# Cross attention with scores by head in 64-row halves, two units of scores and maxima by turns, then the value products of two units

## The chip, the cores and the metric

One core of a Trainium2 chip runs the whole program. The metric is the device time of one execution in microseconds (us), less is better.

## The reference

A two-layer Perceiver-like network on 128 query tokens of width 256, with a context of S = 12544 rows of width 256. The part that the change touches is the cross attention of the second layer, 16 heads of 16 columns:

```python
q, k, v = x @ Wq.T + bq, ctx @ Wq.T + bq, ctx @ Wq.T + bq   # projected by a shared weight
scores  = q_h @ k_h.T * 16 ** -0.5        # for each head h: 128 x 12544, fp32 accuracy
p       = softmax(scores, -1)             # over all 12544 keys
x       = x + concat_h(p @ v_h) @ Wo.T + bo
```

Everything before it (a history context, convolutional attention, kernel attention, a mixture of experts) and after it (a retention layer, a low-rank feed-forward) is the same in both kernels.

## The kernel before

Keys and values were projected earlier and lie in device memory (`k_scratch`, a rounded high part and a low part of each key row; `v_scratch`). The 16 heads are worked in NG = 8 pairs. For pair `s` the keys stand in `k_stack[s % 2]`, a tile of 128 partitions by 12544 keys: head 0 of the pair in rows 0 to 48, head 1 in rows 64 to 111. Its rows are three copies of the head's 16 dimensions (high, low, high) and a row of ones (row 32) which carries the negated maximum of each query into the score. `q_max` and `q_stack` hold the queries in the same rows. All these tiles are fp32r, the rounded 32-bit type; `prob` and `vals` are plain fp32, and a product of them is recorded as two matmuls.

TensorE has three kinds of work for a pair:

- **Maxima** (`maximum_group`, L866): queries stationary, keys moving, units of MU = 448 keys. The two heads of a pair are two matmuls in different row halves, into two PSUM banks. VectorE then takes the maxima of both banks in one reduction of 896 columns (`reduce_unit`, L1616). There are 28 units in a pair and 224 in all. `MAX_SLOTS` holds two slots of two banks, and a unit waits until the reduction of the unit two before it is done.
- **Scores** (`scores`, L889): a tile of 128 keys stationary, all 112 rows at once, and 256 moving columns: 128 for each head, with zeros in the rows of the other head. Two tiles fill one bank, and ScalarE turns that bank of 512 columns into `prob` (`exponentials`, L1180). There are 98 tiles and 49 exponentials in a pair, 784 and 392 in all, in three banks.
- **Value products** (`weigh`, L905): 32 columns of `vals` stationary, 128 columns of `prob` moving, into four column groups of 32 partitions in one bank.

When all units of a pair are reduced, VectorE takes the pair's maximum (L1622), TensorE turns it into rows (`turn_maxima`, L876) and ScalarE copies the row into `q_stack` (L1173); then the scores of the pair may start.

The order on TensorE is written out by `step_plan`. First come 32 units of maxima (the first pair and LEAD = 2 groups of two units), with nothing between them. Then come 131 steps: the scores of STEP = 3 exponentials (6 tiles), the value products of the step before, and a group of two units of maxima, which `due` leaves out in about every seventh step. The last 19 steps have no maxima left. Each engine runs its own instructions in order and waits on counters: `c_max` counts maxima matmuls and `c_red` reductions, `c_sc` scores, `c_exp` exponentials, `c_wt` value products. SyncE loads the keys of pair `s` chunk by chunk as soon as the scores of pair `s - 2` have passed them.

Of the kernel before, what the change touches and what calls it, by code (L numbers as in the profile page):

```python
# [59 lines left out]
MU = 448  # L60
UNITS = S // MU
EU = TILES // 2
# [3 lines left out]
CHUNK_EXPS = EU // CHUNKS  # L66
CHUNK_UNITS = UNITS // CHUNKS
STEP = 3
LEAD = 2
NPB = 12  # L70
# [4 lines left out]
STACK = 112  # L75
MAX_SLOTS, EXP_BANKS, SUM_BANK = (0, 2), (4, 5, 6), 7
# [44 lines left out]

def step_plan():


    half = UNITS // 2
    steps, placed, turned = [], half + LEAD, 1
    for j in range(-(-EXPS // STEP)):
        exps = range(STEP * j, min(STEP * j + STEP, EXPS))
        turns = []
        if turned < NG and placed >= half * (turned + 1):  # L130
            turns.append(turned)
            turned += 1
        due = min(half * NG, half + LEAD + STEP * (j + 1) * half // EU)
        steps.append((exps, turns, range(placed, due)))
        placed = max(placed, due)
    return steps


def pack_columns(parts):
# [28 lines left out]
    ("iota", E), ("pair_rows", 2)])  # L168
# [24 lines left out]
def constants():  # L193
# [13 lines left out]
    for q in range(4):  # L207
        for hh in range(2):
            for d in range(HD):
# [3 lines left out]
                low[src, q, at + 2 * HD + 1 - hh] = 1  # L213
# [3 lines left out]
    put("pair_rows", r[:, None] // 64 == np.arange(2))  # L217
# [25 lines left out]
def build_kernel(nc, k_scratch, v_scratch, ones_scratch, ctx_t, x_in, mask_in, const_in, hist_in, l0_in, rows0_in, xw_in, x_bo_in, x_o_in, l1_in, rows1_in, v_in,  # L243
                 tables_in, out):
    with ExitStack() as outer:  # L245
# [134 lines left out]
        q_stack = sb("q_stack", [P, NG, 2 * T], F32R, scope=le)  # L380
        unit_max = sb("unit_max", [P, 2, UNITS, 2], scope=le)
# [6 lines left out]
        prob = sb("prob", [P, NPB, 2, 2 * T], scope=le)  # L388
# [89 lines left out]
        for exps, turns, groups in step_plan():  # L478
# [8 lines left out]
        def _(sp):  # L487
# [53 lines left out]
            def load_keys(s, c):  # L541

                cols = slice(c * CHUNK, (c + 1) * CHUNK)
                if s >= 2:
                    sp.wait_ge(c_sc, exp_at[EU * (s - 2) + CHUNK_EXPS * (c + 1) - 1][0] + 1)
                for at, which in ((0, 0), (HD, 1)):
# [4 lines left out]
                for hh in range(2):  # L551
                    row, at = 2 * HD * s + HD * hh, 64 * hh + 2 * HD + 1 - hh
                    sp.dma_start(k_stack[s % 2][at:at + HD, cols].bitcast(F32),
                                 k_scratch[0, row:row + HD, cols]).then_inc(c_stack[s % 2][c], 16)
# [8 lines left out]
            def fill(b):  # L563

                sp.dma_start(k_stack[b][MAX_ROW:MAX_ROW + 1, :].bitcast(F32), ones_scratch).then_inc(c_fill[b], 16)
                sp.dma_start(k_stack[b][MAX_ROW + 1 + HD:64, :].bitcast(F32),
                             k_scratch[0, 0:64 - MAX_ROW - 1 - HD, :]).then_inc(c_fill[b], 16)
# [29 lines left out]
        def _(pe):  # L597
# [254 lines left out]
            max_ring = Ring(MAX_SLOTS)  # L852

            def maximum_group(g):

                s = g // (UNITS // 2)
                for u in (2 * g % UNITS, 2 * g % UNITS + 1):
                    n, at = max_ring.take()
                    wait_at(pe, c_red, max_ring.free(n))
                    if u == 0 and s < 2:  # L860
                        pe.wait_ge(c_fill[s], 32)
                    if u % CHUNK_UNITS == 0:
                        pe.wait_ge(c_stack[s % 2][u // CHUNK_UNITS], 96 * (s // 2 + 1))
                    cols = slice(u * MU, (u + 1) * MU)
                    for hh, rows in ((0, slice(0, 3 * HD + 1)), (1, slice(64, 64 + 3 * HD))):
                        last = nc.tensor.matmul(bank[:, at + hh, 0:MU], q_max[rows, s, :], k_stack[s % 2][rows, cols],  # L866
                                                start=True, stop=True)
                    last.then_inc(c_max, 1)
# [43 lines left out]
            for g in range(UNITS // 2):  # L912
                maximum_group(g)
# [847 lines left out]
```

## Time and profile before

| | |
|---|---|
| Runs of the kernel before | median 1046.29 us of three, 1046.09 to 1048.83 |
| The profiled execution | 1046.74 us, span 1044.7 us |
| Granted TensorE clock over the span | 0.879 of full speed |
| First maxima until the first score | 623.8 to 658.9 us |
| Scores, value products and later maxima | 658.9 to 957.2 us |
| What follows the cross attention's loop | 957.2 to 1044.7 us |

In the profile PE is a matmul on TensorE, and PEld the load of its stationary operand; DVE is VectorE, ACT ScalarE, SPq the queue of SyncE. A matmul's record begins when it is issued and holds the wait for its weights and the way to its end, so records overlap: the distance between two starts tells the rate, not the duration. A granted clock of 1.00 is the level of 2.4 GHz, 0.50 that of 1.2 GHz.

### The profile page before, as it was taken

To read this page: it belongs to the slowest core of one execution; us is meant where nothing else is said; L and a number is where in the kernel's file an instruction comes from. 1 tells how busy PE (TensorE), PEld (TensorE's weight loads), DVE (VectorE), ACT (ScalarE), POOL (GpSimd) and SP (SyncE) were. 2 spreads that over 40 slices of the span, in tenths; PEclk is the share of its full clock that TensorE was granted. 3 is DMA by queue.
4 is the path that set the end of the run, shared out by engine and by line. 5 is a ranking of instruction groups with operands and counts; after the bars stand their busy time and mean duration, and the time that the engine had idled before them with its cause. 6 is when DMAs were issued, how large, how long until landed. Compare 5 with 4: busy or idle time off the path is not lost. (4 is left out here: it accounts for less than half of the span.)

```text
span 1044.7 us, 19625 instructions
## 1 busy us (share of the span) xinstructions
PE 859.5 (82%) x7644; PEld 669.5 (64%) x7644; DVE 636.5 (61%) x1132; ACT 541.6 (52%) x1075; POOL 127.8 (12%) x135
## 2 busy tenths in 40 slices
PE   4999999999999997360065957999999999998756
PEld 4888878788787884240042942677777777776544
DVE  3555566677666676639933449677778778731141
ACT  2776777867768676130021100566666666675010
POOL 2322222222222220008000000000000000000010
PEclk9999999999999998685556885799999999999575
DMA  3465644555545555240029269479979988341000
GB/s 111 129 167 155 173 119 145 135 159 148 144 136 142 134 144 95 104 199 0 0 29 145 42 127 209 85 128 185 190 158 176 179 180 154 96 147 58 1 0 5
DMA packets 83138, 126.26 MB, mean 121 GB/s; under 512 B 10755, under 2 KB 73476, under 8 KB 82246
## 3 DMA queue, kind: packets, MB, share of 16 engines
q1 hardware_dynamic: 83046, 125.01, 50.1%
q8 instruction: 60, 0.98, 0.4%
q14 instruction: 32, 0.26, 0.1%
HBM read 85.46 MB, written 39.52 MB: 120 GB/s over the span
## 5 line engine op out<-in xcount | busy, mean ns | idle before, releaser
L1616 DVE TENSOR_REDUCE unit_max<-bank 128x2 f32<-128x896 f32 x224 | 232.4, 1085 | 64.5 <-PE bank L866 64.3
L1180 ACT ACTIVATE prob<-bank 128x512 f32<-128x512 f32 x392 | 205.8, 598 | 82.4 <-PE bank L889 79.4
L889 PE MATMUL bank<-q_stack,k_stack 112*128 112x256 f32 x784 | 129.2, 300 | 0.7 <-ACT q_stack L1173 0.5
L601 PE MATMUL bank<-hc_high,w_high 128*128 128x256 f32 x392 | 117.6, 300 | 8.6 <-POOL hc_low L1234 8.4
L889 PEld LDWEIGHTS bank<-q_stack,k_stack 112*128 112x128 f32 x784 | 102.3, 190 | 31.5 <-ACT prob L1180 17.6
L1349 DVE SCALAR_TENSOR_TENSOR normed<-bank,b_centered,rstd_wide 128x256 f32<-128x256 f32 x196 | 85.4, 478 | 46.8 <-ACT rstd_wide L1060 46.6
L905 PE MATMUL bank<-prob,vals 128*32 128x128 f32 x3136 | 113.4, 278 | 0.0
L601 PE MATMUL bank<-hc_high,w_low 128*128 128x256 f32 x392 | 112.6, 287 | 0.0
L601 PE MATMUL bank<-hc_low,w_high 128*128 128x256 f32 x392 | 112.3, 286 | 0.0
L866 PE MATMUL bank<-k_stack,q_max 49*128 49x448 f32 x448 | 95.8, 484 | 12.5 <-DVE unit_max L1616 11.1
L1053 ACT ACTIVATE square<-bank,b_centered 128x256 f32<-128x256 f32 x196 | 81.8, 471 | 28.5 <-PE bank L601 28.5
L646 PE MATMUL bank<-eh,hw 128*128 128x512 f32 (+1 forms) x200 | 92.7, 588 | 0.0
L905 PEld LDWEIGHTS bank<-prob,vals 128*32 128x32 f32 x3136 | 78.1, 110 | 17.5 <-ACT prob L1180 0.4
L601 PEld LDWEIGHTS bank<-hc_high,w_high 128*128 128x128 f32 x392 | 76.4, 195 | 9.3 <-issue 9.3
L866 PEld LDWEIGHTS bank<-k_stack,q_max 49*128 49x128 f32 x448 | 43.1, 198 | 54.6 <-DVE unit_max L1616 32.6
L601 PEld LDWEIGHTS bank<-hc_high,w_low 128*128 128x128 f32 x392 | 76.8, 196 | 0.0
L601 PEld LDWEIGHTS bank<-hc_low,w_high 128*128 128x128 f32 x392 | 76.2, 194 | 0.0
L1045 ACT ACTIVATE eh<-normed,hw 128x512 f32<-128x512 f32 (+1 forms) x100 | 74.4, 806 | 0.1
L601 PE MATMUL bank<-hc_high,x_high 128*128 128x256 f32 x196 | 73.1, 373 | 0.0
L1250 POOL TENSOR_TENSOR rstd<-var_eps,half_power 128x1 f32<-128x1 f32 x8 | 4.4, 550 | 552.7 <-DVE var_eps L1408 552.7
L1372 DVE CUSTOM_DVE_ANT_0 eh<-eh,logits 128x1024 f32<-128x1024 f32 (+1 forms) x52 | 59.4, 1161 | 17.2 <-POOL h_rstd L1239 13.8
L1234 POOL TENSOR_TENSOR hc_low<-hc_raw,hc_high 128x512 fp32r<-128x512 f32 x49 | 62.4, 1273 | 46.4 <-DVE group_stats L1372 45.2
(299 smaller groups left out, 1287.4 us busy)
## 6 DMA issues: line engine op xcount, KB each, us to landing
k_stack<-k_scratch SPq DMA_DIRECT2D x336, 112.0 KB, 5.1
vals<-v_scratch SPq DMA_DIRECT2D x8, 1666.0 KB, 10.3
v_scratch<-vst SPq DMA_DIRECT2D x12, 1088.0 KB, 9.5
hc_raw<-in_ctx_t SPq DMA_DIRECT2D x49, 256.0 KB, 3.1
k_scratch<-k_high SPq DMA_DIRECT2D x49, 256.0 KB, 3.4
k_scratch<-k_low SPq DMA_DIRECT2D x49, 256.0 KB, 3.5
w_ffn<-in_l SPq DMA_DIRECT2D x4, 1920.0 KB, 13.8
w_l<-in_l SPq DMA_DIRECT2D x6, 603.0 KB, 5.4
```

The costliest lines, as they stand in the source:

```text
L601: last = nc.tensor.matmul(out_ap, lhs, rhs, start=(n == 0), stop=(n == len(pairs) - 1))
L646: last = nc.tensor.matmul(bank[:, 5, 0:width], w1_hist[:, c, :], eh[:, gb, c, at:at + width], start=(c == 0), stop=(c == CT - 1))
L866: last = nc.tensor.matmul(bank[:, at + hh, 0:MU], q_max[rows, s, :], k_stack[s % 2][rows, cols], start=True, stop=True)
L889: last = nc.tensor.matmul(bank[:, at, t * 2 * T:(t + 1) * 2 * T], k_stack[s % 2][0:STACK, k * P:(k + 1) * P], q_stack[0:STACK, s, :], star ...
L905: last = nc.tensor.matmul(bank[at:at + 32, SUM_BANK, 0:T], vals[:, s % 2, hh, k * VW:k * VW + 32], prob[:, e % NPB, t, hh * T:(hh + 1) * T ...
L1045: A(eh[:, group % 2, c, at:at + width], normed[:, i % 2, c, 0:width], ACT.Gelu, bias=v_hist["beta"][:, c:c + 1], scale=v_hist["g"][:, c:c ...
L1053: ins = A(square[:, c, :], bank[:, 2 * (n % 2) + half, (c % 2) * CH:(c % 2 + 1) * CH], ACT.Square, bias=b_centered[:, c:c + 1])
L1180: A(prob[:, e % NPB, :, :], bank[:, at, :].rearrange("p (u t) -> p u t", u=2), ACT.Exp).then_inc(c_exp, 1)
L1234: TT(hc_low[:, b], hc_raw[:, b], hc_high[:, b].bitcast(F32), ALU.subtract).then_inc(h_low, 1)
L1349: V.scalar_tensor_tensor(out=normed[:, n // 2 % 2, c, at:at + CH], in0=bank[:, 2 * b + half, (c % 2) * CH:(c % 2 + 1) * CH], scalar=b_cent ...
L1372: V.tensor_tensor_reduce(part_of, part_of, logits[:, gb, lo:lo + width], 1.0, 0.0, ALU.mult, ALU.add, group_stats[:, group, half * CT + c: ...
L1616: V.tensor_reduce(unit_max[:, s % 2, u, :], bank[:, at:at + 2, 0:MU], AX_X, ALU.max, negate=True).then_inc(c_red, 1)
```

## The change

Each head gets its own ones row (rows 32 and 96), and each head's scores become a matmul of its own with 49 rows in its own row half, as the maxima have it. The moving operand of a score is then 128 columns in place of 256, and there are two matmuls for each tile of keys. A unit is now four tiles or 512 keys for both kinds of work: 24 whole units and one of two tiles in a pair, 25 in place of 28 (maxima) and 49 (exponentials). An exponential covers two banks, 1024 columns, in two slots. The maxima have three single banks, and VectorE reduces each head's bank by itself, 512 columns, 400 reductions in all. A step is: scores of a unit, maxima of a unit, scores, maxima, and then the value products of the two units of the step before. 30 units of maxima stand ahead of the first score.

```diff
-MU = 448
-UNITS = S // MU
-EU = TILES // 2
+UT = 4
+UK = UT * P
+EU = -(-TILES // UT)
-STEP = 3
-LEAD = 2
-NPB = 12
+STEP = 2
+LEAD = 5
+NPB = 6
-STACK = 112
-MAX_SLOTS, EXP_BANKS, SUM_BANK = (0, 2), (4, 5, 6), 7
+HEAD_ROWS = 3 * HD + 1
+MAX_BANKS, EXP_BANKS, SUM_BANK = (0, 1, 2), (3, 5), 7
...
-            def maximum_group(g):
...
+            head_rows = [slice(64 * hh, 64 * hh + HEAD_ROWS) for hh in range(2)]
+
+            def maximum(m):
+
+                s, u = divmod(m, EU)
+                wait_at(pe, c_red, 2 * m + 2 - len(MAX_BANKS))
...
+                for hh in range(2):
+                    at = MAX_BANKS[(2 * m + hh) % len(MAX_BANKS)]
+                    nc.tensor.matmul(bank[:, at, 0:hi - lo], q_max[head_rows[hh], s, :],
+                                     k_stack[s % 2][head_rows[hh], lo:hi], start=True, stop=True).then_inc(c_max, 1)
...
-                for t in range(2):
-                    k = 2 * u + t
-                    last = nc.tensor.matmul(bank[:, at, t * 2 * T:(t + 1) * 2 * T],
-                                            k_stack[s % 2][0:STACK, k * P:(k + 1) * P], q_stack[0:STACK, s, :],
-                                            start=True, stop=True)
+                for t, k in enumerate(unit_tiles(u)):
+                    for hh in range(2):
+                        last = nc.tensor.matmul(bank[:, at + hh, t * T:(t + 1) * T],
+                                                k_stack[s % 2][head_rows[hh], k * P:(k + 1) * P],
+                                                q_stack[head_rows[hh], s, :], start=True, stop=True)
                 last.then_inc(c_sc, 1)
...
-            for exps, turns, groups in step_plan():
+            for exps, turns in step_plan():
                 for e in exps:
                     scores(e)
+                    if e + EU + LEAD < EXPS:
+                        maximum(e + EU + LEAD)
...
-            for hh in range(2):
-                ins = V.tensor_scalar(by_pair(q_stack[:, :, hh * T:(hh + 1) * T]), stacked, pair_rows[:, hh:hh + 1],
-                                      None, ALU.mult)
-                link(ins) if hh == 0 else done(ins, "q_stack")
+            done(V.tensor_copy(by_pair(q_stack[:, :, :]), stacked), "q_stack")
...
+                for hh in range(2):
+                    at = MAX_BANKS[(2 * m + hh) % len(MAX_BANKS)]
+                    dve.wait_ge(c_max, 2 * m + hh + 1)
+                    V.tensor_reduce(unit_max[:, s % 2, u, hh:hh + 1], bank[:, at, 0:width], AX_X, ALU.max,
+                                    negate=True).then_inc(c_red, 1)
```

On TensorE, the first steps of the loop in the kernel before, after the maxima that stand ahead of it (a count at a row's end is that of calls; a value product is recorded twice):

```order
L866 MATMUL bank<-k_stack,q_max 128x448 x64
L876 MATMUL bank<-const,neg_max 32x128 x2
L889 MATMUL bank<-q_stack,k_stack 128x256 x12
L905 MATMUL bank<-prob,vals 32x128 x12
L866 MATMUL bank<-k_stack,q_max 128x448 x4
L889 MATMUL bank<-q_stack,k_stack 128x256 x6
L905 MATMUL bank<-prob,vals 32x128 x12
L866 MATMUL bank<-k_stack,q_max 128x448 x4
```

Three kinds of work follow each other once in every step of six tiles. On TensorE a step of the changed kernel in the running loop (L883 are its scores, L860 its maxima, L898 its value products):

```order
L883 MATMUL bank<-q_stack,k_stack 128x128 x8
L860 MATMUL bank<-k_stack,q_max 128x512 x2
L883 MATMUL bank<-q_stack,k_stack 128x128 x8
L860 MATMUL bank<-k_stack,q_max 128x512 x2
L898 MATMUL bank<-prob,vals 32x128 x16
L883 MATMUL bank<-q_stack,k_stack 128x128 x8
L860 MATMUL bank<-k_stack,q_max 128x512 x2
```

The units of maxima are now parted by scores alone or by scores and value products; a step holds eight tiles, and the 16 calls of value products are those of the two units of the step before.

On VectorE, from the query tiles on, before:

```order
L1602 CAST q_max<-bank 128x4x2x128
L1604 TENSOR_SCALAR q_stack<-bank,const 128x4x2x128 x2
L1616 TENSOR_REDUCE unit_max<-bank 128x2 x28
L1622 TENSOR_REDUCE neg_max<-unit_max 128x2
```

and in the changed kernel:

```order
L1594 CAST q_max<-bank 128x4x2x128
L1595 CAST q_stack<-bank 128x4x2x128
L1606 TENSOR_REDUCE unit_max<-bank 128x1 x50
L1612 TENSOR_REDUCE neg_max<-unit_max 128x2
```

One of the two long writes of `q_stack` is gone, and 28 reductions of a pair become 50 shorter ones.

## Rows read from the trace of the kernel before

**Rows 1.** The page: busy time, share of the span, instructions of each engine.

```profile
PE 859.5 (82%) x7644; PEld 669.5 (64%) x7644; DVE 636.5 (61%) x1132; ACT 541.6 (52%) x1075; POOL 127.8 (12%) x135
```

**Rows 2.** Stretches: us, busy time (count) by engine, granted clock, DMA share, GB/s.

```profile
450.00:560.00 110.00, 38.73 (x136) 24.57 (x135) 67.31 (x154) 18.12 (x50) 23.47 (x21) 0.61 0.19 43
...
623.80:658.90 35.10, 23.88 (x68) 9.44 (x68) 34.76 (x35) 0.39 (x2) 0.00 (x0) 0.55 0.86 178
...
665.00:922.00 257.00, 254.32 (x3694) 185.44 (x3696) 198.59 (x196) 175.64 (x341) 0.00 (x0) 1.00 0.78 154
922.00:957.30 35.30, 34.91 (x613) 27.29 (x602) 2.98 (x4) 30.68 (x60) 0.00 (x0) 1.00 0.45 151
...
624.00:628.00 4.00, 0.91 (x6) 0.37 (x4) 3.93 (x4) 0.00 (x0) 0.00 (x0) 0.92 1.00 179
628.00:632.00 4.00, 2.98 (x10) 1.15 (x8) 4.00 (x5) 0.00 (x0) 0.00 (x0) 0.50 1.03 186
```

**Rows 3.** Who waited for whom, 655 to 955 us: total, times, longest.

```profile
DVE unit_max L1616 <- PE bank L866: 64.3, 92, 6.1
...
PEld bank L866 <- DVE unit_max L1616: 10.0, 46, 1.0
PEld bank L876 <- DVE neg_max L1622: 4.6, 7, 0.7
```

**Rows 4.** Timeline of two steps of the running loop: start, length, engine, work.

```profile
753.55 0.83 PE L866 MATMUL bank<-k_stack,q_max 49*128 49x448 f32 x4
753.91 0.18 PEld L866 LDWEIGHTS bank<-k_stack,q_max 49*128 49x128 f32 x2 [0.18 <-DVE unit_max L1616]
...
754.31 0.77 PEld L889 LDWEIGHTS bank<-q_stack,k_stack 112*128 112x128 f32 x6 [0.21 <-issue]
...
754.85 1.57 ACT L1180 ACTIVATE prob<-bank 128x512 f32<-128x512 f32 x3 [0.88 <-PE bank L889]
755.21 0.59 PEld L905 LDWEIGHTS bank<-prob,vals 128*32 128x32 f32 x24
...
756.00 0.39 PEld L866 LDWEIGHTS bank<-k_stack,q_max 49*128 49x128 f32 x4 [0.20 <-issue]
...
756.52 2.09 DVE L1616 TENSOR_REDUCE unit_max<-bank 128x2 f32<-128x896 f32 x2 [0.36 <-PE bank L866]
...
758.30 0.19 PEld L866 LDWEIGHTS bank<-k_stack,q_max 49*128 49x128 f32 x2 [0.20 <-issue]
...
758.66 0.19 PEld L866 LDWEIGHTS bank<-k_stack,q_max 49*128 49x128 f32 x2 [0.17 <-DVE unit_max L1616]
```

**Rows 5.** Timeline of the maxima ahead of the loop, and its first score.

```profile
623.77 2.60 DVE L1604 TENSOR_SCALAR q_stack<-bank,const 128x1024 fp32r<-128x1024 f32 x2
...
632.54 0.74 PE L866 MATMUL bank<-k_stack,q_max 49*128 49x448 f32 x2 [0.26 <-DVE unit_max L1616]
...
656.73 0.74 PE L866 MATMUL bank<-k_stack,q_max 49*128 49x448 f32 x2 [0.26 <-DVE unit_max L1616]
...
658.92 1.65 PE L889 MATMUL bank<-q_stack,k_stack 112*128 112x256 f32 x6 [0.46 <-ACT q_stack L1173]
```

**Rows 6.** Timeline: value products of 40 records, then two steps without maxima.

```profile
703.55 1.03 PEld L905 LDWEIGHTS bank<-prob,vals 128*32 128x32 f32 x40
...
704.78 0.30 PEld L866 LDWEIGHTS bank<-k_stack,q_max 49*128 49x128 f32 x4 [0.20 <-issue]
...
936.49 0.77 PEld L889 LDWEIGHTS bank<-q_stack,k_stack 112*128 112x128 f32 x6 [0.20 <-ACT prob L1180]
...
938.18 0.78 PEld L889 LDWEIGHTS bank<-q_stack,k_stack 112*128 112x128 f32 x6 [0.20 <-ACT prob L1180]
```

**Rows 7.** TensorE's weight loads alone, in the window 754.77 to 754.88 us.

```profile
754.77 0.30 PEld L889 LDWEIGHTS bank<-q_stack,k_stack 112*128 112x128 f32 x2
```

**Rows 8.** Groups by form: line, shapes, count, busy us, mean ns, idle before.

```profile
L1496 DVE TENSOR_REDUCE s_max<-conv 128x4 f32<-128x512 f32 x1 | 0.7, 686 | 0.0
...
L866 PE MATMUL bank<-k_stack,q_max 49*128 49x448 f32 x192 | 72.6, 445 | 0.4 <-DVE unit_max L1616 0.4
```

More of the change, by code:

```diff
@@ L119, in free, with unit_tiles @@
         return n - len(self.banks) + 1
+def unit_tiles(u):
+    return range(UT * u, min(UT * u + UT, TILES))
 def step_plan():
-    half = UNITS // 2
-    steps, placed, turned = [], half + LEAD, 1
+    steps, placed, turned = [], EU + LEAD, 1
     for j in range(-(-EXPS // STEP)):
@@ L129, in step_plan @@
         turns = []
-        if turned < NG and placed >= half * (turned + 1):
+        if turned < NG and placed >= EU * (turned + 1):
             turns.append(turned)
             turned += 1
-        due = min(half * NG, half + LEAD + STEP * (j + 1) * half // EU)
-        steps.append((exps, turns, range(placed, due)))
-        placed = max(placed, due)
+        steps.append((exps, turns))
+        placed = min(EXPS, placed + len(exps))
     return steps
@@ L544, in load_keys @@
                 if s >= 2:
[L545 to L546 removed]
+                    sp.wait_ge(c_sc, exp_at[EU * (s - 2) + ((c + 1) * CHUNK - 1) // UK][0] + 1)
+                for at, which in ((0, 0), (HD, 1), (2 * HD + 1, 0)):
                     for hh in range(2):
@@ L875, in turn_maxima @@
                 for hh in range(2):
-                    last = nc.tensor.matmul(bank[MAX_ROW:MAX_ROW + 32, at, hh * T:(hh + 1) * T],
-                                            neg_max[:, hh, :].bitcast(F32), ident, start=True, stop=True)
+                    row = 64 * hh + MAX_ROW
+                    last = nc.tensor.matmul(bank[row:row + 32, at, 0:T], neg_max[:, hh, :].bitcast(F32), ident,
+                                            start=True, stop=True)
                 last.then_inc(c_sc, 1)
@@ L929, in _ @@
                     turn_maxima(s)
-                for g in groups:
-                    maximum_group(g)
             for e in waiting:
                 weigh(e)
-            pe.wait_ge(c_red, NG * UNITS)
+            pe.wait_ge(c_red, 2 * EXPS)
             for g in range(NG):
@@ L1188, in _ @@
             ready = None
-            for exps, turns, groups in step_plan():
+            for exps, turns in step_plan():
                 for e in exps:
@@ L1623, in reduce_unit @@
                                     ALU.min).then_inc(c_hm, 1)
-            for s in range(NG):
-                for u in range(UNITS):
-                    reduce_unit(s, u)
+            for m in range(EXPS):
+                reduce_unit(m)
             dve.wait_ge(c_ot, 1)
```

83 lines of the change are left out of this document (31 added, 52 removed).

## Prediction, made before the run

> **What bounds the kernel now.** The page first: TensorE is busy for 82% of the span, no other engine for more than 61% [rows 1]. The stretches then give the stages. In the loop of the cross attention, 665 to 922 us, TensorE has work for 254.3 of 257.0 us at clock 1.00, while VectorE has it for 198.6 and ScalarE for 175.6 us; from 922 us, where no maxima are left, it is 34.9 of 35.3 us [rows 2]. So the loop lasts as long as TensorE's instructions and its short waits. The maxima ahead of the loop, 623.8 to 658.9 us, are another matter: VectorE has 34.8 of 35.1 us, TensorE 23.9 at clock 0.55 [rows 2]. There VectorE is the bound. In the list of waits TensorE loses 10.0 us in the loop to reductions and 4.6 to a pair's maximum, and VectorE waits 64.3 us for maxima [rows 3]: the two engines are close to each other and linked both ways.
>
> The timeline of two steps shows the pieces of 12 key tiles in 4.75 us (753.55 to 758.30) [rows 4]. Starts of weight loads give: maxima of two units 0.76 and then 0.61 us (the first with a wait for VectorE in it, 0.18 us), six scores 0.90 us (754.31 to 755.21), 24 value products 0.79 us (755.21 to 756.00). A short window shows the fifth load of the scores at 754.77 [rows 7], 0.46 us after the first: 0.115 us from one to the next. Five such distances make 0.58 us of the block's 0.90, and 0.32 us pass from the last load to the next kind of work, some 0.2 us more than a distance: that is the price of a change of kind. A step without maxima takes 1.69 us (936.49 to 938.18) [rows 6].
>
> **What the change takes away.** Before, a cycle of seven steps (42 tiles) is three times 4.75 us and one step of 1.69: 15.94 us, or 3.04 us for eight tiles. The 112 steps that have maxima or are such a seventh one make 255.0 us, the 19 last ones 32.1: together 287.1 of the 298.3 us from the first score (658.92, rows 5) to the loop's end at 957.2. The other 11.2 us are turns of maxima and the slow clock at the start.
>
> **What it puts there, by TensorE's own work.** A score is now two matmuls of 128 columns in two row halves. The maxima already show such pairs: two heads' weight loads are recorded together, 0.18 us for both [rows 4]. I price a pair of scores by its weights at 0.12 us, as one score now. Below, it can't be less than that load. Above, no row has an fp32r matmul under 256 columns; the nearest row is that of plain fp32, four value products of 128 columns in (1.23 - 0.79) / 4 = 0.11 us for each of the two records of a product [rows 4, 6], so 0.22 us for the whole. I take 0.12: the maxima are fp32r matmuls of 49 rows like the new scores, and with 448 columns they take 0.445 us, their wait for weights in it [rows 8], where fp32's rate would make 0.77 us of the columns alone (448 x 0.22 / 128). The 32 value product records of eight tiles take 0.79 + 8 x 0.0275 = 1.01 us.
>
> **What it puts in the way.** This decides. With three single banks, unit m+1 waits for 2m+1 reductions: the first reduction of unit m itself must be over. Before, a unit waited for the one two before it. So between two units of maxima stands a closed loop: load and matmul to the start of the reduction 0.52 us (756.00 to 756.52) and 0.03 for 64 more columns; a reduction of 512 columns 0.69 us (686 ns in another reduction of that width, rows 8); 0.05 us until TensorE goes on (reductions that end at 758.61, loads of the next unit at 758.66). That is 1.29 us. The scores of one unit between them need TensorE for only about 0.8 us, so it stands still for 0.5 us, and the value products are queued behind the waiting maxima, and the exponentials' next scores behind these.
>
> From the second unit to the first of the next step: maxima to value products 0.40 (753.91 to 754.31) + 0.03 = 0.42; value products 1.01; four pairs of scores until the next load 0.46 (the fifth of the loads at 754.31 + 0.46). In these 1.89 us VectorE catches up. A step is 1.29 + 1.89 = 3.18 us, against 3.04 before for the same eight tiles: two changes of kind in eight tiles in place of four are worth less than the wait.
>
> **The sum.** 85 steps with maxima: 270.3, less 3 for six half units. 15 steps without: scores 0.81 + 0.32 - 0.05, products 1.01, so 2.09 each, 31 in all. Of the 11.2 us of turns and start I keep 5: a pair's last unit is now placed a whole step (3 us) before its turn, so the 4.6 us of waits go, and the two turning matmuls go to two column groups, some 1.5 us. Loop: 303 against 298.3, **+5**.
>
> Ahead of the loop: 32 reductions one behind the other took 1.0 us each (the units that they release start from 632.54 to 656.73, 24 distances, rows 5). Now 28 distances between 30 units are the closed loop again. At 1.2 GHz a unit's matmul takes 0.74 us [rows 5], 0.79 for 512 columns, so the loop is 0.79 + 0.05 + 0.69 + 0.05 = 1.58 us; at 2.4 GHz 1.29. The granted clock was 0.92 in 624 to 628 us and 0.50 in 628 to 632 [rows 2], with TensorE mostly waiting, and I expect the same: 2 x 1.29 + 26 x 1.58 - 0.5 = 43.2. The reductions start some 1.3 us earlier, at 625.1 in place of 626.4, since one of the two long writes of `q_stack` (2.60 us, rows 5) is gone; the last unit is issued at about 669, where it was 656.73, **+12**. VectorE alone would allow some 0.6 us a reduction (1.0 us for 896 columns, by width), 1.2 a unit, but its speed isn't the limit.
>
> Hidden: ScalarE's exponential of 1024 columns costs at most twice the 0.485 us by which three follow each other [rows 4], 1.94 us a step. The key loads are as many and as large in a longer loop (DMA share 0.78 now, rows 2), and their lead, 20 units of 25, is about as long; the second row of ones is loaded well ahead. If a load came late, the maxima would wait, and behind them all of TensorE.
>
> Sum: 1046.7 + 12 + 5 = **1064 us** on the profiled execution's time, which is 0.4 us above the median of the runs. Everything outside stays.
>
> The Trainium skill (TensorE: Matmul & The Clock Gate, Back-to-back issue gap) gives about 81 ns for each 128-column matmul in a stream with its weights. My row has 0.12 us for a load of 128 fp32r columns, and goes before it. By the page a step would be some 0.14 us shorter behind the value products, and the sum 1052.
>
> **Rivals.**
> *Scores of 128 columns at fp32's rate, or row halves that don't overlap.* Either makes a pair cost 0.22 to 0.24 us. The closed loop hides it between its two units (1.2 of 1.29 us), behind the value products it adds 0.40 us, to 85 steps 34 us; in the 15 last steps 0.87 each, 13 us: 1111 us. For it: no fp32r matmul so narrow is in the trace. Against: the maxima overlap in their row halves. The Trainium skill (FP8 and Floating Point Precision, TensorE Precision Notes) says that true FP32 takes four passes; the rows of value products agree (0.22 us for 128 columns), and no run here shows if a narrow fp32r matmul falls to it.
>
> *Faster: the wait for the own unit's reduction doesn't bind.* Then a step is TensorE's work: 0.32 + 0.36 us from unit to unit, 2.57 a step, 52 us less in the loop, and ahead of it 30 x 1.2 us of reductions, 9 us less: 1003. The sign turns where the closed loop is below 1.09 us in the loop. For it: three changes of kind in six tiles become two in eight. Against: the awaited count, and TensorE's starts 0.05 us behind reductions [rows 4, 5].
>
> *The clock.* TensorE will stand for 0.5 us in every 3.18. In 450 to 560 us, where it had 38.7 of 110 us, 0.61 was granted; and 0.55 ahead of the loop, where it had 23.9 of 35.1 [rows 2]. At the lower level throughout, a step would be near 5 us and the sum 1220; for half of the loop 1144. Against: it keeps work for about 85% of a step.
>
> *No difference*, if the first stage keeps the full clock (8 us less) and scores are as cheap as the page says (12 less).
>
> **How the numbers follow.** Forecast 0.58 (its own range 1052 to 1073), narrow scores slow 0.24, clock 0.06, faster 0.05, no difference 0.04, the rest slower for another reason. A change under 0.3%, 3 us, can't be told from none here. The range 1052 to 1113 holds the first two. Faster 0.05, same 0.04, slower 0.91.
>
> **What would show it.** Steps of 3.2 us, with TensorE's idle time put down to the maxima's reduction, about 0.5 us in each; no such wait ahead of value products. First score at 671, after units 1.58 us apart at clock 0.50. Loads of score pairs 0.12 us apart; at 0.22 the first rival holds. Clock 1.00 in the loop. I am wrong if steps are 2.6 us, or if the waits go to keys or exponentials.

## The result, and the profile after

The changed kernel takes 1093.32 us (median of four runs, 1092.65 to 1096.68); beside it the kernel before took 1047.56 (1046.09 to 1051.41, four runs). The ratio is 1.044, with a 95% interval of 1.040 to 1.0475: slower by 46 us. The forecast was 1064 us: the direction is right, the size is not (17 us more than before were forecast). The range of 1052 to 1113 us holds the time, but by luck: the forecast's own part of it ends at 1073, and what lies above was there for slow narrow scores, which the trace doesn't show. Here and below a run more than 1.5% above the fastest of its kernel counts as slow (three of e2_order, three of e6_both, one of e4_warm), and medians, ranges and ratios are those of the other runs.

The page of the changed kernel, first its engines and then TensorE's clock in 40 slices of 27 us (9 is full speed, 5 half of it):

```profile
PE 867.4 (79%) x8380; PEld 687.8 (63%) x8380; DVE 655.6 (60%) x1307; ACT 530.3 (49%) x891; POOL 127.8 (12%) x135
...
PEclk9999999999999998755557855557999999999566
```

TensorE works 8 us longer than before [rows 1] in a span that is 46.3 us longer. The rest is time in which it stands. The second stretch of four slices at 5 in the row of the clock is 627 to 736 us: the maxima ahead of the cross attention's loop, and the loop's first 60 us.

The stretches of the changed kernel: the maxima ahead of the loop, the loop's start, its running part, and its end without maxima (columns as in [rows 2]):

```profile
629.20:676.30 47.10, 23.46 (x64) 8.50 (x64) 39.38 (x62) 0.56 (x3) 0.00 (x0) 0.54 0.52 108
676.30:748.40 72.10, 71.46 (x732) 54.61 (x736) 38.44 (x62) 32.34 (x34) 0.00 (x0) 0.50 0.45 87
748.40:968.00 219.60, 192.89 (x3588) 149.16 (x3584) 176.61 (x283) 137.43 (x155) 0.00 (x0) 1.00 0.72 153
968.00:1003.70 35.70, 34.10 (x765) 28.36 (x766) 1.01 (x4) 29.45 (x34) 0.00 (x0) 1.00 0.43 150
```

Three things are to be seen. The stage ahead of the loop takes 47.1 us in place of 35.1, and VectorE, which had work for all of it [rows 2], now stands for 8 of them. In the running part TensorE has work for 192.9 of 219.6 us, where it was 254.3 of 257.0. And in the first 72 us of the loop the granted clock is 0.50, the level of 1.2 GHz, although TensorE is recorded as busy for 71.5 of the 72.1 us. Before, the clock was 1.00 from 665 us on, 6 us behind the first score.

The account, by the places that both traces share:

| | before | after | difference |
|---|---|---|---|
| start until the first maxima | 623.8 | 629.2 | +5.4 |
| first maxima until the first score | 35.1 | 47.1 | +12.0 |
| first score until the loop's end | 298.3 | 327.4 | +29.1 |
| what follows | 87.5 | 87.3 | -0.2 |
| span | 1044.7 | 1091.0 | +46.3 |

The timeline of one running step, at clock 1.00 (start, length, engine, work, and in brackets the wait ahead of it):

```profile
802.43 0.52 PEld L883 LDWEIGHTS bank<-q_stack,k_stack 49*128 49x128 f32 x8 [0.20 <-issue]
...
802.87 0.19 PEld L860 LDWEIGHTS bank<-k_stack,q_max 49*128 49x128 f32 x2
...
802.98 0.65 PEld L883 LDWEIGHTS bank<-q_stack,k_stack 49*128 49x128 f32 x8
...
803.41 2.57 DVE L1606 TENSOR_REDUCE unit_max<-bank 128x1 f32<-128x512 f32 x4 [0.60 <-PE bank L860]
...
804.15 0.19 PEld L860 LDWEIGHTS bank<-k_stack,q_max 49*128 49x128 f32 x2 [0.52 <-DVE unit_max L1606]
...
804.59 0.81 PEld L898 LDWEIGHTS bank<-prob,vals 128*32 128x32 f32 x32 [0.25 <-issue]
...
805.60 0.19 PEld L883 LDWEIGHTS bank<-q_stack,k_stack 49*128 49x128 f32 x2 [0.20 <-issue]
```

From 802.43 to 805.60 a step is 3.17 us. Its two units of maxima are 1.28 us apart (802.87, 804.15), and the second waited 0.52 us for a reduction. Nothing waits ahead of the value products (0.25 us for issue only). The list of waits for 676 to 968 us adds it up (total, times, longest):

```profile
DVE unit_max L1606 <- PE bank L860: 76.1, 97, 2.6
...
PEld bank L860 <- DVE unit_max L1606: 40.3, 86, 0.7
...
PE bank L860 <- DVE unit_max L1606: 26.4, 67, 0.6
```

Loads of the maxima wait 86 times for a reduction, 40.3 us, where it was 46 times and 10.0 us [rows 3]. Only 3.6 of the 40.3 us lie in the stretch at the low clock: there TensorE's own work between two units takes nearly as long as the wait. The third row is the same wait as the matmuls behind those loads record it, and isn't added.

### The profile page after: what moved, and what is told of

The parts are those of the page before. It is cut to its first block and busy times, and to the rows that moved or that the text cites. A ratio compares the mean times of both kernels' runs of the same rounds, so it can differ in the third digit from the quotient of the medians.

```text
span 1091.0 us, 20902 instructions
## 1 busy us (share of the span) xinstructions
PE 867.4 (79%) x8380; PEld 687.8 (63%) x8380; DVE 655.6 (60%) x1307; ACT 530.3 (49%) x891; POOL 127.8 (12%) x135
## 5 line engine op out<-in xcount | busy, mean ns | idle before, releaser
L1606 DVE TENSOR_REDUCE unit_max<-bank 128x1 f32<-128x512 f32 (+1 forms) x400 | 252.6, 675 | 84.1 <-PE bank L860 83.6
L1174 ACT ACTIVATE prob<-bank 128x1024 f32<-128x1024 f32 (+1 forms) x200 | 192.5, 1005 | 119.2 <-PE bank L883 118.4
L860 PE MATMUL bank<-k_stack,q_max 49*128 49x512 f32 (+1 forms) x400 | 111.4, 553 | 51.7 <-DVE unit_max L1606 49.4
L883 PEld LDWEIGHTS bank<-q_stack,k_stack 49*128 49x128 f32 x1568 | 121.5, 207 | 29.7 <-issue 20.3
L883 PE MATMUL bank<-q_stack,k_stack 49*128 49x128 f32 x1568 | 132.4, 293 | 1.7 <-ACT prob L1174 1.1
L898 PE MATMUL bank<-prob,vals 128*32 128x128 f32 x3136 | 118.2, 296 | 0.5 <-issue 0.5
L898 PEld LDWEIGHTS bank<-prob,vals 128*32 128x32 f32 x3136 | 87.4, 118 | 26.1 <-issue 22.3
L1044 ACT ACTIVATE square<-bank,b_centered 128x256 f32<-128x256 f32 x196 | 81.8, 471 | 29.1 <-PE bank L596 29.1
L860 PEld LDWEIGHTS bank<-k_stack,q_max 49*128 49x128 f32 x400 | 44.0, 217 | 79.1 <-DVE unit_max L1606 77.3
```

The source lines that it names most:

```text
L860: nc.tensor.matmul(bank[:, at, 0:hi - lo], q_max[head_rows[hh], s, :], k_stack[s % 2][head_rows[hh], lo:hi], start=True, stop=True).then_i ...
L883: last = nc.tensor.matmul(bank[:, at + hh, t * T:(t + 1) * T], k_stack[s % 2][head_rows[hh], k * P:(k + 1) * P], q_stack[head_rows[hh], s, ...
L898: last = nc.tensor.matmul(bank[at:at + 32, SUM_BANK, 0:T], vals[:, s % 2, hh, k * VW:k * VW + 32], prob[:, e % NPB, hh, t * T:(t + 1) * T] ...
L1044: ins = A(square[:, c, :], bank[:, 2 * (n % 2) + half, (c % 2) * CH:(c % 2 + 1) * CH], ACT.Square, bias=b_centered[:, c:c + 1])
L1174: A(prob[:, e % NPB, :, 0:width], bank[:, at:at + 2, 0:width], ACT.Exp).then_inc(c_exp, 1)
L1606: V.tensor_reduce(unit_max[:, s % 2, u, hh:hh + 1], bank[:, at, 0:width], AX_X, ALU.max, negate=True).then_inc(c_red, 1)
```

## The experiments

Two questions are open: does the awaited count of reductions cost what the prediction said, and what held the clock down for 72 us? Each edit is to the changed kernel unless it says otherwise. Times are medians. "Low start" is the time from the first score until the clock is 1.00, in the one profiled run of each kernel; a step is two units of four tiles, at full clock. All runs come first, in one table, then each by itself. The kernel before ran again beside each group of them, with medians of 1050.9, 1051.4 and 1051.1 us.

| kernel | step, us | low start, us | median, us | ratio to before (95%) |
|---|---|---|---|---|
| changed kernel | 3.17 | 72 | 1093.3 | 1.044 (1.040 to 1.0475) |
| e1_split | 3.17 | 72 | 1085.4 | 1.032 (1.028 to 1.037) |
| e2_order | 2.72 | 28 | 1050.8 | 1.002 (0.998 to 1.005) |
| e3_short | 2.77 | 49 | 1049.6 | one run |
| e4_warm | 3.17 | see text | 1088.6 | 1.039 (1.034 to 1.0435) |
| e5_wide | 3.39 | 16 | 1092.8 | 1.0405 (1.036 to 1.045) |
| e6_both | 2.72 | 28 | 1042.0 | 0.990 (0.987 to 0.993) |
| e7_before_wait | 3.76 | on and off | 1279.7 | one run |
| e9_rows64 | 2.72 | 14 | 1030.0 | 0.981 (0.973 to 0.9885) |
| e12_rows64_again | 2.72 | 14 | 1034.0 | 0.986 (0.982 to 0.989) |
| e10_rows_only | 3.17 | 14 | 1068.4 | 1.017 (1.012 to 1.022) |
| e11_wide_both | 3.00 | 9 | 1050.7 | 0.999 (0.998 to 1.000) |

### One wait for each bank (e1_split)

```diff
-                wait_at(pe, c_red, 2 * m + 2 - len(MAX_BANKS))
...
                 for hh in range(2):
+                    wait_at(pe, c_red, 2 * m + hh + 1 - len(MAX_BANKS))
```

Before the edit both matmuls of a unit wait for the count that the second needs; now each waits for its own bank's reduction.

> The changed kernel with one edit: each of a unit's two maxima matmuls waits for the reduction that frees its own bank, so the first no longer waits for the unit's predecessor. Theory A (the closed loop of matmul and reduction paces the maxima ahead of the loop, and the loop step holds one such wait whichever matmul carries it): ahead of the loop units come every 1.2 us and not 1.57, the first score some 10 us earlier, steps of the running loop stay at 3.17 us, the low clock at the start of the loop stays: 1082 us. Rival B (the low clock in the first steps is inherited from a long starved stage ahead of the loop): the clock rises earlier too, and the time falls to 1065 or less. Rival C (VectorE's own speed is the limit ahead of the loop): no change, 1093 us.

Measured: 1085.4 us (1080.87 to 1089.16). The stage ahead of the loop is 37.4 us long (628.2 to 665.6), 9.7 shorter. Its timeline shows one matmul at a time, each behind a reduction:

```profile
650.56 0.28 PEld L860 LDWEIGHTS bank<-k_stack,q_max 49*128 49x128 f32 x1 [0.32 <-DVE unit_max L1606]
...
651.16 0.28 PEld L860 LDWEIGHTS bank<-k_stack,q_max 49*128 49x128 f32 x1 [0.31 <-DVE unit_max L1606]
```

They are 0.60 us apart: 1.2 us a unit in place of 1.57, which is what VectorE's reductions alone allow. So the awaited count was all but 2.3 of the 12 us in this stage. In the loop nothing changes: steps 3.165 us, 72 us at the low clock. There the second head's matmul still has to wait for the same reduction, and the value products are queued behind it. The clock fell once more near the end (983.4 to 1000 us), and in the profiled run (1088.96 us) the loop took some 7 us longer than in the changed kernel.

### Value products between the two units of maxima (e2_order)

```diff
             for exps, turns in step_plan():
+                ahead = [e + EU + LEAD for e in exps if e + EU + LEAD < EXPS]
                 for e in exps:
                     scores(e)
-                    if e + EU + LEAD < EXPS:
-                        maximum(e + EU + LEAD)
+                for m in ahead[:1]:
+                    maximum(m)
...
                     turn_maxima(s)
+                for m in ahead[1:]:
+                    maximum(m)
```

Two scores, a unit of maxima, the value products, a unit of maxima: the 1.01 us of value products now stand between units.

> The changed kernel with the order of a step altered and nothing else: scores, scores, maxima, value products, maxima. Theory A (the 0.5 us in each step are the wait for the reduction of the unit just before, and the low clock in the first 70 us of the loop comes from TensorE waiting in each slow step): value products or two units of scores now stand between any two units of maxima and cover 1.29 us, steps of 2.6 to 2.7 us, the clock at 1.00 within 10 us of the first score, 1020 to 1030 us. Rival D (the low clock has nothing to do with the waits): steps of 2.65 us once the clock is up, but the slow stretch stays, 1045 to 1055 us. Rival E (row halves and changes of kind cost what they cost, order is nothing): 1090 us.

Measured: 1050.8 us, seven runs from 1046.15 to 1060.17, where theory A had 1020 to 1030 and rival D 1045 to 1055. A step at full clock is 2.72 us, 0.45 less than in the changed kernel, and the maxima's matmuls wait 2.7 us for reductions in the whole loop (26.4 in the changed kernel). The stretches of the profiled run (span 1054.7) show two parts at the low clock all the same:

```profile
674.10:702.10 28.00, 27.22 (x288) 21.51 (x288) 14.56 (x24) 12.87 (x13) 0.00 (x0) 0.50 0.40 72
702.10:879.60 177.50, 171.72 (x3243) 135.12 (x3243) 161.03 (x259) 124.58 (x142) 0.00 (x0) 1.00 0.90 185
879.60:903.40 23.80, 22.83 (x253) 17.98 (x255) 11.27 (x19) 9.16 (x11) 0.00 (x0) 0.50 0.61 103
```

This confirms the prediction's step: the wait is a matter of what stands between two units, and it goes when the order changes. It doesn't confirm that the wait alone holds the clock down: here TensorE had work for 27.2 of 28.0 us, and the clock was low.

### Short reductions (e3_short)

```diff
-                    V.tensor_reduce(unit_max[:, s % 2, u, hh:hh + 1], bank[:, at, 0:width], AX_X, ALU.max,
+                    V.tensor_reduce(unit_max[:, s % 2, u, hh:hh + 1], bank[:, at, 0:P], AX_X, ALU.max,
```

This kernel leaves out three quarters of the maxima: VectorE reduces 128 of 512 columns.

> The changed kernel in its own order, with each reduction taking the maxima of 128 of the 512 columns (this leaves three quarters of the maxima out). Theory A: a reduction takes 0.29 us in place of 0.69, so the closed loop falls to about 0.9 us and under TensorE's own work between two units. Units ahead of the loop every 1.15 us, steps of 2.6 to 2.75 us, almost no wait for reductions, the clock at 1.00 soon after the first score, 1015 to 1030 us. Rival D: the slow stretch at the start of the loop stays, 1045 us.

Measured: 1049.6 us (one run; theory A had 1015 to 1030), steps of 2.77 us. The order is that of the change, so its waits go when VectorE is quick: the closed loop holds. The two stretches at the low clock:

```profile
662.30:711.60 49.30, 49.30 (x540) 39.49 (x542) 10.96 (x45) 23.76 (x23) 0.00 (x0) 0.50 0.46 81
...
841.30:861.80 20.50, 20.50 (x246) 16.40 (x244) 4.61 (x19) 9.71 (x12) 0.00 (x0) 0.51 0.57 98
```

TensorE is recorded as busy for 49.30 of 49.30 and 20.50 of 20.50 us, and has 0.50. After this run "TensorE waits, therefore the clock is low" can't stand as the sole cause.

### A burst ahead of the first score (e4_warm)

```diff
             turn_maxima(0)
+            for _ in range(5):
+                nc.tensor.matmul(bank[:, SUM_BANK, :], ident, const[:, 0:512], start=True, stop=True)
```

Five plain fp32 products of 128 rows and 512 columns, which nothing uses.

> The changed kernel with five plain fp32 matmuls of 512 columns (no use is made of them) between the turn of the first pair and the first score, 6 to 9 us of unbroken work for TensorE. Theory A (the loop can hold the full clock with its waits, and only fails to reach it): the clock is at 1.00 from the first steps on, steps of 3.17 us throughout, the 14 slow steps of 5.02 us gone: 27 us less for some 7 more, 1073 us. Rival F (the loop's waits pull the clock down again while maxima and scores are new): it falls back to 0.50 within a few steps, 1095 to 1100 us.

Measured: 1088.6 us (three runs, 1087.84 to 1093.36), some 5 us under the changed kernel. How much of that is the burst's isn't shown: in the profiled run the first maxima came 4.8 us earlier than in the changed kernel's (624.4), the burst took 6 us more ahead of the first score, and the loop was 6 us shorter. The burst in the timeline, and the stretches behind it:

```profile
670.73 7.00 PE L909 MATMUL bank<-const 128*128 128x512 f32 x10
```

```profile
675.60:682.40 6.80, 5.64 (x48) 3.35 (x46) 3.76 (x6) 3.75 (x4) 0.00 (x0) 0.99 0.00 0
682.40:730.20 47.80, 47.40 (x512) 36.32 (x510) 24.25 (x40) 19.08 (x21) 0.00 (x0) 0.50 0.50 88
...
744.00:965.00 221.00, 194.21 (x3624) 150.45 (x3626) 177.68 (x286) 138.44 (x156) 0.00 (x0) 1.00 0.75 151
```

The burst brought the clock to 1.00 at 675.6 us, and the loop's own work lost it again within 5 us of the burst's end. So the low stretch isn't a late start that one must only get over: the loop's work at that place doesn't keep the clock. Later it does, with the same steps: from 730.2 us on, but for one fall of 3.4 us, the clock is 1.00.

### The scores of before in the units and the order of the change (e5_wide)

```diff
-                    for hh in range(2):
-                        last = nc.tensor.matmul(bank[:, at + hh, t * T:(t + 1) * T],
-                                                k_stack[s % 2][head_rows[hh], k * P:(k + 1) * P],
-                                                q_stack[head_rows[hh], s, :], start=True, stop=True)
+                    last = nc.tensor.matmul(bank[:, at + t // 2, t % 2 * 2 * T:(t % 2 + 1) * 2 * T],
+                                            k_stack[s % 2][0:STACK, k * P:(k + 1) * P], q_stack[0:STACK, s, :],
+                                            start=True, stop=True)
```

With it come one shared row of ones and `q_stack` with zeros as before, and `prob` with the two heads side by side. Banks, units, waits and order are those of the change.

> The changed kernel with the scores of the kernel before put back (112 rows, 256 moving columns, one matmul for a tile of keys), in the changed kernel's units, banks and order. Theory G (two matmuls of 128 columns leave TensorE's array idle during half of each pair's weight load, and that holds the granted clock down): the clock is at 1.00 within 10 us of the first score and stays there, in spite of the wait for reductions. Steps are then 3.4 us (1.29 + 0.42 + 1.01 + 0.67: a change of kind more on each side of the scores), the time 1080 to 1088 us. Theory A (the waits hold the clock down): it stays at 0.50 for 50 us or more, 1105 us or above.

Measured: 1092.8 us (1092.45 and 1093.13), where 1080 to 1088 was expected. Its stretches:

```profile
677.70:693.70 16.00, 15.98 (x104) 10.94 (x104) 7.73 (x12) 7.41 (x7) 0.00 (x0) 0.51 0.24 44
693.70:970.00 276.30, 266.49 (x3565) 183.96 (x3568) 207.55 (x334) 168.90 (x176) 0.00 (x0) 1.00 0.67 141
```

The low start is 16 us in place of 72, though the waits for reductions are all there. So the narrow scores (more matmuls, fewer rows and columns in each) are part of the clock's cause. That the time is the same as the changed kernel's comes from two opposite terms: a step is 3.387 us in place of 3.166 (some 19 us over 85 steps), and the clock gives some 20 us. Order and waits are equal, so the 0.22 us are what the narrow scores take out of a step. They lie between the value products and the next maxima. Four tiles of narrow scores take 0.44 us there (802.43 to 802.87 in the timeline above), the maxima following them as work of the same kind; four wide ones take 0.66, with a change of kind behind them:

```profile
805.05 0.53 PEld L887 LDWEIGHTS bank<-q_stack,k_stack 112*128 112x128 f32 x4 [0.20 <-issue]
...
805.71 0.19 PEld L866 LDWEIGHTS bank<-k_stack,q_max 49*128 49x128 f32 x2
```

Between the two units of maxima wide scores cost nothing more (1.28 us apart, 805.71 to 806.99): there they only shorten the wait.

### The wait of the change in the kernel before (e7_before_wait)

Edit to the kernel before, a unit waits for the one just before it:

```diff
                     n, at = max_ring.take()
-                    wait_at(pe, c_red, max_ring.free(n))
+                    wait_at(pe, c_red, n)
```

> The kernel before with one edit: a unit of maxima waits for the reduction of the unit just before it, and not of the one two before. Closed loop at either level of the clock: ahead of the loop a unit every 1.9 us (1.0 before), in the loop the second unit of a group 1.65 us behind the first (0.36 before), so steps with maxima last 3.7 us, some 160 us more in all: 1200 us. Theory A: with a third of each step spent waiting the clock stays at 0.50 for long at the start of the loop or falls in it, 1230 us or more. Theory G: with the wide scores kept the clock is up soon after the first score and holds, 1195 to 1210 us.

Measured: 1279.7 us (one run), above what either theory had as its range or bound (1195 to 1210; 1230 or more). At full clock a step with maxima is 3.755 us (3.7 was expected), but the clock goes up and down all the way:

```profile
699.60:1180.00 480.40, 367.42 (x4052) 253.92 (x4054) 208.84 (x197) 195.26 (x379) 0.00 (x0) 0.78 0.42 93
```

The timeline of a group shows what it waits for:

```profile
905.42 0.74 PE L866 MATMUL bank<-k_stack,q_max 49*128 49x448 f32 x2
...
907.35 0.74 PE L866 MATMUL bank<-k_stack,q_max 49*128 49x448 f32 x2 [1.19 <-DVE unit_max L1616]
```

With waits of 1.19 us in each group and TensorE at work for 367 of 480 us, the clock falls again and again though the scores are wide. So both things count: how long TensorE stands, and what the work is that it has.

### Both cures of the wait (e6_both)

The edits of e1_split and e2_order together.

> The changed kernel with both edits: the order scores, scores, maxima, value products, maxima, and each maxima matmul waiting for its own bank. By the closed loop: a unit every 1.27 to 1.43 us at the low clock ahead of the loop, 8 to 10 us less than with the order alone, steps of 2.72 us at the full clock and 4.72 at the low one. Theory G: the low stretches come as with the order alone, 1036 to 1050 us, and vary from run to run. Were the clock up from the start and throughout, it would be 1018 us.

Measured: 1042.0 us, seven runs from 1033.41 to 1045.49; this is already 1% under the kernel before. The two edits add up: the stage as in e1_split, the step as in e2_order. So the waits of the change can be cured without giving up its scores, and what is left is the clock. The stage ahead of the loop is 37.3 us, a step 2.716 us. The clock is low in two stretches (and in 781.5 to 784.9 us):

```profile
661.40:689.40 28.00, 27.62 (x290) 21.78 (x290) 14.34 (x23) 12.90 (x13) 0.00 (x0) 0.51 0.43 72
...
866.90:890.80 23.90, 23.76 (x265) 18.80 (x266) 11.88 (x21) 9.32 (x12) 0.00 (x0) 0.51 0.58 100
```

### 64 rows in place of 49 (e10_rows_only)

```diff
-HEAD_ROWS = 3 * HD + 1
+HEAD_ROWS = 64
...
+                for hh in range(2):
+                    row = 64 * hh + 3 * HD + 1
+                    sp.dma_start(k_stack[b][row:64 * hh + 64, :].bitcast(F32),
+                                 k_scratch[0, 0:64 - 3 * HD - 1, :]).then_inc(c_fill[b], 16)
```

Scores and maxima of each head take all 64 rows of its row half. The 15 added rows hold keys of other heads, loaded once, and zeros on the queries' side, so they add nothing to a score. Instructions, columns, order and waits are those of the changed kernel.

> The changed kernel with one edit: scores and maxima run over all 64 rows of their half in place of 49 (the 15 more rows hold finite keys against queries of zero). Times of single instructions and waits stay as they are. Theory H (rows in use count for the granted clock): the slow stretch at the start of the loop gets shorter than 72 us, some 3.7 us less for each two slow steps gone, 1065 to 1080 us. Theory G (only streaming counts, rows don't): the same stretch of 12 or 13 slow steps, 1093 us.

Measured: 1068.4 us (1064.26 and 1072.43), 25 us less than the changed kernel, from one number and the two loads that go with it. The two runs differ by 8 us, and the profiled one is the slower. The stretches:

```profile
676.10:690.10 14.00, 13.87 (x132) 10.89 (x134) 7.79 (x13) 7.36 (x7) 0.00 (x0) 0.50 0.31 50
690.10:967.00 276.90, 244.46 (x4604) 190.28 (x4602) 208.03 (x335) 177.97 (x202) 0.00 (x0) 1.00 0.73 157
```

The first score starts at 676.1 (676.3 in the changed kernel) and a step is 3.166 us as there; what differs is that the clock rises after 14 us in place of 72 and stays. So what stands in the 15 further rows of a half bears on when the full clock is granted. Whether it is the number of rows or the keys that move through them isn't shown: no run filled the rows on both sides with zeros. The changed kernel wasn't run beside e10_rows_only; e9_rows64 below makes the same step beside its twin e6_both.

### 64 rows with both cures (e9_rows64 and e12_rows64_again)

The edits of e10_rows_only and e6_both together; e12_rows64_again is the same kernel in another comparison.

> The kernel with both edits, and in addition all 64 rows of each half in use by scores and maxima (the 15 more rows hold finite keys against queries of zero). No instruction more on any engine but two small loads. Theory G in the form that only streaming counts: no difference from the kernel with both edits. Theory H (rows in use count for the granted clock): it rises sooner and the dip in the middle of the loop goes, 1018 to 1030 us.

> The kernel with both edits and all 64 rows once more, for an interval: 1024 to 1036 us, 1.5 to 2.3% under the kernel before. Theory H says that it stays under the kernel with both edits and 49 rows (1043 us); if its two runs were luck, it comes out at 1040 to 1045.

Measured: 1030.0 us (1024.05 and 1035.93), and again 1034.0 (four runs, 1031.18 to 1038.54), a ratio of 0.986 (0.982 to 0.989). It is under the kernel before by 1.1 to 1.8%. Against e6_both, which ran beside e9_rows64 and has 49 rows, the low start is 14 us in place of 28, and the time 12 us less. The stretches of the second profile:

```profile
662.10:675.80 13.70, 13.34 (x130) 10.58 (x130) 6.53 (x11) 7.03 (x7) 0.00 (x0) 0.50 0.29 51
675.80:860.20 184.40, 180.82 (x3401) 147.03 (x3399) 163.55 (x271) 130.52 (x148) 0.00 (x0) 1.00 0.91 185
860.20:873.80 13.60, 13.26 (x147) 10.19 (x147) 6.44 (x10) 4.90 (x5) 0.00 (x0) 0.51 0.65 115
```

One dip of 13.6 us is left in the middle of the loop; in the first profile it was one of 3.4 us (800.4 to 803.8). The two profiled runs of this one kernel differ by such dips.

### Wide scores with both cures (e11_wide_both)

The edits of e5_wide and e6_both together.

> The scores of the kernel before in the changed kernel's units and banks, with the order scores, scores, maxima, value products, maxima and each maxima matmul waiting for its own bank. No closed loop in a step, but four changes of kind in eight tiles: 1.13 + 0.42 + 1.01 + 0.42 = 2.98 us a step (2.72 with scores in row halves). Theory G: with wide scores the clock is up within some 16 us of the first score and never dips, 1040 to 1048 us, and from run to run it varies less than the kernel with narrow scores. If wide scores don't matter for the clock, dips as in that kernel and 1050 us or more.

Measured: 1050.7 us in eight runs from 1048.96 to 1051.46, the same as before (ratio 0.999); 1040 to 1048 had been expected for a clock without dips. A step is 2.997 us (2.98 was expected). The stretches:

```profile
667.80:676.80 9.00, 8.64 (x56) 6.12 (x56) 3.77 (x6) 5.12 (x5) 0.00 (x0) 0.51 0.19 42
676.80:962.00 285.20, 284.39 (x4230) 210.53 (x4234) 212.30 (x341) 190.36 (x210) 0.00 (x0) 1.00 0.71 156
```

9 us at the low clock, no dip, and a spread of 2.5 us, where the narrow twin e6_both has 12 us. With e6_both it shows the narrow scores by themselves in a schedule without waits: 0.28 us less in a step, and a clock that comes and goes.

## Why the prediction was right in part and wrong in size

**What bounds it, and the step: right.** The step was worked out at 3.18 us and is 3.17. Its terms, predicted and measured: from unit to unit 1.29 and 1.28; maxima to value products 0.42 and 0.44; value products 1.01 and 1.01; scores until the next load 0.46 and 0.44. TensorE stands 0.52 us in each step at full clock, 40.3 us in all, at the maxima's load alone. e2_order and e3_short take the closed loop apart from either side (more work in it, a shorter reduction), and the step falls to 2.72 and 2.77.

**Ahead of the loop: right.** 12 us more were predicted and 12.0 are there; the units start 1.57 us apart (1.58 predicted). e1_split shows the cause by taking it away: 9.7 us less. The timeline of the changed kernel there:

```profile
655.89 0.80 PE L860 MATMUL bank<-k_stack,q_max 49*128 49x512 f32 x2 [0.78 <-DVE unit_max L1606]
...
657.46 0.80 PE L860 MATMUL bank<-k_stack,q_max 49*128 49x512 f32 x2 [0.78 <-DVE unit_max L1606]
```

The first score came at 676 and not 671, since the stage began 5.4 us later.

**Narrow scores: right.** Four pairs of loads and then the maxima's begin from 802.43 to 802.87, 0.11 us from pair to pair, so neither half of the first rival holds; 0.12 was taken. (The row of [rows 7] is of the window that begins at 754.88; its start, 754.77, is what the argument uses.) The Trainium skill (TensorE: Matmul & The Clock Gate, Back-to-back issue gap) has 81 ns for one matmul of 128 columns with its weights. The trace doesn't agree: 0.11 us for a pair is more than one such matmul by that figure and less than two.

**The clock in the loop: the step that failed.** The prediction said "Clock 1.00 in the loop" and gave the rival of the clock 0.06, against it "it keeps work for about 85% of a step". The loop's first 72.1 us went at 0.50. Steps take 5.02 us there in the trace, as that rival had worked out ("near 5 us"). 72.1 us hold 14.4 such steps, which at 3.17 us are 45.6: this costs **26 us**. The other 3 us of the loop's +29.1 stand against the +5 of the forecast, in whose sum the slow start and the turns of the maxima together had 5 us. The experiment that comes nearest to taking it away alone is e10_rows_only: with 14 us of low clock in place of 72 it takes 1068.4 us, 4 us from the forecast of 1064 (some 5 us for the 14 slow ones, and about as much for a late start of the stage, are in it). The rival had asked the wrong question. It looked at the share of time in which TensorE has work, and that share speaks the other way in the changed kernel: 99% in the stretch at 0.50 (71.46 of 72.10), 88% in the one at 1.00 (192.89 of 219.60). So the share of work doesn't tell the clock here; what the work is matters too: two matmuls of 49 rows and 128 columns where there was one of 112 rows and 256 columns. e5_wide (wide scores, all waits: 16 us), e10_rows_only (64 rows, all waits: 14 us), e2_order (49 rows, hardly a wait: 28 us) and the changed kernel (49 rows and waits: 72 us) show that either cure shortens the low start. How far it is the waits themselves stays open, since e3_short has none in its first 49 us and is at 0.50 all the same; e2_order also has another order. The Trainium skill (TensorE: Matmul & The Clock Gate, HAM oscillation — how this bites in real kernels) lays a clock that falls again and again to gaps in TensorE's work, waits for DMA in its example. e7_before_wait agrees in kind (waits of 1.19 us for reductions, 0.78 granted over 480 us); e3_short doesn't, with 49.3 us at 0.50 and no gap recorded.

**Changes of kind: right in the counting, high in the price.** The prediction priced one at some 0.2 us and counted two in a step of the changed kernel (to the value products and back), since scores and maxima are now alike. e5_wide, where they are unlike, has a step 0.22 us longer by one change, and what it adds between the two units lies in the wait; e11_wide_both against e6_both, without waits and with two more changes in a step, gives 0.28, or 0.14 for one.

**The 5.4 us ahead of the stage** weren't predicted, and they are a difference of runs and not of kernels. The first maxima start at 623.8 to 624.7 us in the profiled runs of before, e4_warm, e6_both, e7_before_wait and e12_rows64_again, and at 626.6 to 629.7 in all others. e12_rows64_again (624.7) and e9_rows64 (629.7) are the same kernel. The traces that start early have a stretch at full clock from 552 or 553 to 559 or 560 us which the late ones lack. The kernel before differs by as much from run to run: its 39 runs beside the experiments go from 1046.3 us at a granted clock of 0.879 to 1052.6 at 0.874. So some 5 of the 46.3 us between the two profiled spans need not be the change's. What brings the early stretch isn't known.

**What stays open.** Why the clock in the loop rises when it does (72 us in the changed kernel at nearly the same steps that later hold it for 220 us), and why kernels with narrow scores and few waits dip once more in the loop (879.6 in e2_order, 841.3 in e3_short, 866.9 in e6_both, 860.2 in e12_rows64_again; e1_split, with its waits, at 983.4) while the two with wide scores in the new units (e5_wide, e11_wide_both) don't. The runs tell which kernels it meets, not its rule.

## What to carry to other kernels

When buffers become fewer or of another size, write down which completion each wait now names and what work stands between the two ends of that closed loop: here that gave 3.18 us for a step of 3.17, and moving 1.01 us of other work between the two units took 0.45 us out of it. When matmuls become smaller, ask the clock's question apart from the wait's question: a TensorE that is recorded as busy may still be at 1.2 GHz, and 15 more rows in each half, which add nothing to a score, cost no time in a step and gave 25 us. Test the parts of a change before it is given up: scores by halves with the waits cured and the rows filled take 1030 to 1034 us, against 1051 for the kernel before in the same comparisons.

## What the runs showed of the hardware

- **Rows in use bear on the clock.** 49 to 64 rows of each half (the further ones with keys against zeros), instructions and order equal: the low stretch behind the first score went from 72 to 14 us, the time from 1093.3 to 1068.4 us (e10_rows_only); with the waits cured from 28 to 14 us (e6_both, e9_rows64).
- **The clock was low with TensorE busy.** 49.30 of 49.30 us at 0.50 in e3_short; 27.62 of 28.00 in e6_both.
- **A burst doesn't last.** Ten dense fp32 matmul records over 7.0 us brought the clock from 0.50 to 0.99, and it fell back 5 us after they ended (e4_warm).
- **A narrow fp32r matmul isn't slow.** Pairs of 49 rows and 128 columns in two row halves follow each other every 0.11 us.
- **VectorE can work one bank at a time without loss.** Reductions of 512 columns start 0.60 us apart, where 896 columns took 1.0 us: the same per column to 5%.
